# Closing stage of a layer-norm, linear-attention and mixture-of-experts kernel: shared-down and attention products per token tile, and the order of the closing sums

## What is computed

```python
x = L0_attn_x                                   # (1, 1024, 256) float32
xn = _layernorm(x, axis=-1)
x = x + _L0_attn_ref(xn, ...) + _L0_ffn_ref(xn, ...)

# attention: q, k, v = split(xn @ w_qkv); q, k = elu(.) + 1, 16 heads of 16
# running_kv, running_ksum = scans over time of k * v and k, with a decay per head
out = q * running_kv / den
out = out.transpose(0, 2, 1, 3).reshape(B, T, Hid) @ w_out

# feed-forward: each token goes to the best of 8 experts, and all go through a shared one
routed = (h @ wd of the token's expert, gate applied to its input)
shared = _silu_mul(x @ shared_gate_up) @ shared_down
return (routed + shared)
```

## Time and profile before

| | us |
|---|---|
| median of 3 runs | 133.48 |
| lowest and highest of them | 133.03 to 133.86 |
| profiled execution, its own time | 132.86 |
| its span, first to last instruction | 131.2 |
| TensorE busy | 124.0 (94%) |
| VectorE busy | 76.2 (58%) |
| ScalarE busy | 50.6 (39%) |
| GpSimd busy | 31.4 (24%) |

### The profile page before, as it was taken

How to read it: one execution, slowest core, us unless ns; L and a number is a source line. 1 busy time by engine, 2 the same in 40 slices (tenths; PEclk the granted TensorE clock), 3 DMA queues, 4 the chain that set the end, 5 groups by cost and what they waited for, 6 DMA issues and landing times.

```text
span 131.2 us, 2388 instructions
## 1 busy us (share of the span) xinstructions
PE 124.0 (94%) x830; PEld 107.5 (82%) x830; DVE 76.2 (58%) x157; ACT 50.6 (39%) x99; POOL 31.4 (24%) x53
## 2 busy tenths in 40 slices
PE   4989999999999999999999999999999999999870
PEld 1258758787888588999998999899999989999670
DVE  0898876999999967783838333635531324023090
ACT  1675796799856445231313131372222231000000
POOL 7803000018887000101010020202020202478300
PEclk9999999999999999999999999999999999999997
DMA  3675999999942202069999999998881111033336
GB/s 102 206 253 114 315 362 226 227 356 386 387 164 80 90 0 65 20 142 311 334 409 362 370 315 322 371 347 285 303 252 40 38 57 50 9 111 106 94 125 200
DMA packets 20036, 27.25 MB, mean 208 GB/s; under 512 B 1356, under 2 KB 16884, under 8 KB 20024
## 3 DMA queue, kind: packets, MB, share of 16 engines
q1 hardware_dynamic: 14056, 21.24, 50.5%
q0 software_dynamic: 1344, 3.43, 8.2%
q10 hardware_dynamic: 4624, 2.43, 6.6%
HBM read 19.90 MB, written 7.19 MB: 206 GB/s over the span
## 4 chain that ended last, share of the span: by engine, by line
PE 86%; DMA 6%; issue 2%; DVE 2%; POOL 1%; ACT 0%; SPq 0%; DVEq 0%; POOLq 0%
PE ps L1042 21%; PE ps L286 10%; PE ps L285 10%; PE ps L287 10%; PE ps L1056 9%; DMA gu<-in_L_ffn_w_gate_up_dram 6%; PE ps L911 5%; PE ps L986 4%; PE ps L917 4%; PE ps L924 4%; PE ps L980 3%; PE ps L972 2%; PE ps L857 1%; DVE x_sb L840 1%; PE ps L963 1%
## 5 line engine op out<-in xcount | busy, mean ns | idle before, releaser
L1042 PE MATMUL ps<-xgT,gu 128*128 128x144 f32 x256 | 34.2, 287 | 0.6 <-DMA gu<-in_L_ffn_w_gate_up_dram 0.6
L1042 PEld LDWEIGHTS ps<-xgT,gu 128*128 128x128 f32 x256 | 32.3, 190 | 1.2 <-issue 1.0
L794 DVE TENSOR_TENSOR wqkv<-rz,ps 128x288 f32<-128x288 f32 x16 | 7.3, 454 | 26.4 <-ACT rz L545 26.3
L418 POOL DMA_DIRECT2D sorted_rows<-yrow x9 | 6.3, 697 | 60.5 <-DVE yrow L789 55.8
L1056 PE MATMUL ps<-wqkv,dn 128*128 128x144 f32 x128 | 17.4, 289 | 0.0
L545 ACT ACTIVATE rz<-ps 128x288 f32<-128x288 f32 x16 | 6.6, 410 | 26.5 <-PE ps L1042 26.5
L1056 PEld LDWEIGHTS ps<-wqkv,dn 128*128 128x128 f32 x128 | 16.1, 190 | 0.0
L410 POOL DMA_INDIRECT sorted_rows<-xn,slot_row x8 | 11.2, 1397 | 19.2 <-ACT xn L483 17.7
L285 PE MATMUL ps<-xT_hi,sgu_hi 128*128 128x512 f32 x32 | 13.0, 405 | 0.0
L287 PE MATMUL ps<-xT_hi,sgu_lo 128*128 128x512 f32 x32 | 12.5, 391 | 0.0
L286 PE MATMUL ps<-xT_lo,sgu_hi 128*128 128x512 f32 x32 | 12.5, 390 | 0.0
(11 more groups left out here) (146 smaller groups left out, 217.8 us busy)
## 6 DMA issues: line engine op xcount, KB each, us to landing
gu<-in_L_ffn_w_gate_up_dram SPq DMA_DIRECT2D x8, 1024.0 KB, 6.1
dn<-in_L_ffn_w_down_dram SPq DMA_DIRECT2D x8, 512.0 KB
sorted_rows<-zeros SPq DMA_DIRECT2D x1, 2592.0 KB, 16.7
wqkv<-sorted_rows SPq DMA_DIRECT2D x10, 144.0 KB
sorted_rows<-yrow POOLq DMA_DIRECT2D x9, 144.0 KB, 4.0
sgu<-_ffn_shared_gate_up_dram SPq DMA_DIRECT2D x1, 1024.0 KB, 6.1
rden_rows<-rden ACTq DMA_DIRECT2D x1, 1024.0 KB, 14.0
ksum<-rden_rows ACTq DMA_DIRECT2D x2, 512.0 KB, 8.1
```

What stands on the lines that cost most here:

```text
L794: V.tensor_tensor(hr[:, 2 * h:2 * h + 2, :].rearrange("p f s -> p (f s)"), act_sb[:, h, 0:2 * SLOTS], ps[:, 2 * h + 1, 0:2 * SLOTS], ALU.m ...
L1042: ins = mm(ps[:, 2 * h + u, (f % 2) * SLOTS:(f % 2 + 1) * SLOTS], gu[p][:, kc, col:col + P], xgT[:, kc, :], start=(kc == 0), stop=(kc == K ...
```

## The change

TensorE: the two loops become one. For each token tile the 12 shared-down matmuls are followed by the 6 attention matmuls of that tile. The two waits that stood ahead of the second loop stand ahead of the joined one.

VectorE: the order of the 16 closing sums is written out. Tiles 0 to 5 take the dense sum first and then the rows sum, tiles 6 and 7 the rows sum first. The sum that comes first increments `s_sum`, the second `s_fin`, so that each tile is still stored after its second sum. The order is: dense 0, 1, 2, rows 0, dense 3, rows 1, 2, dense 4, rows 3, 4, dense 5, rows 5, 6, dense 6, rows 7, dense 7. The numbers of matmuls, sums, gathers and stores stay as they were.

```diff
-            for i in range(NT + TH):
-                if i < NT:
-                    dve.wait_ge(s_gather[i], 16)
-                    V.tensor_tensor(x_sb[:, i, :], x_sb[:, i, :], y_tok[:, i, :], ALU.add).then_inc(s_sum, 1)
-                if i >= TH:
-                    dve.wait_ge(s_acc, i - TH + 1)
-                    dve.wait_ge(s_sum, i - TH + 1)
-                    V.tensor_tensor(x_sb[:, i - TH, :], x_sb[:, i - TH, :], ps[:, i - TH, 0:D], ALU.add).then_inc(s_fin, 1)
+            ROWS_FIRST = NT - 2
+
+            def dense_add(i):
+
+                dve.wait_ge(s_acc, i + 1)
+                if i >= ROWS_FIRST:
+                    dve.wait_ge(s_sum, i + 1)
+                V.tensor_tensor(x_sb[:, i, :], x_sb[:, i, :], ps[:, i, 0:D], ALU.add).then_inc(s_fin if i >= ROWS_FIRST else s_sum, 1)
+
+            def rows_add(i):
+
+                dve.wait_ge(s_gather[i], 16)
+                if i < ROWS_FIRST:
+                    dve.wait_ge(s_sum, i + 1)
+                V.tensor_tensor(x_sb[:, i, :], x_sb[:, i, :], y_tok[:, i, :], ALU.add).then_inc(s_sum if i >= ROWS_FIRST else s_fin, 1)
+
+            for i in range(3):
+                dense_add(i)
+            rows_add(0)
+            dense_add(3)
+            rows_add(1)
+            rows_add(2)
+            dense_add(4)
+            rows_add(3)
+            rows_add(4)
+            dense_add(5)
+            rows_add(5)
+            rows_add(6)
+            dense_add(6)
+            rows_add(7)
+            dense_add(7)
@@
             pe.wait_ge(s_shl, LAST)
-            pe.wait_ge(s_plo, 1)
+            pe.wait_ge(s_plo, 2)
+            pe.wait_ge(s_attl, KC)
             for i in range(NT):
@@
                 shared_down(i, range(FC))
-            pe.wait_ge(s_plo, 2)
-            pe.wait_ge(s_attl, KC)
-            for i in range(NT):
                 attention_out(i)
```

## The result

| | median us (lowest to highest, runs) |
|---|---|
| before | 134.19 (132.57 to 137.25, 23) |
| changed | 133.34 (131.88 to 137.05, 23) |
| ratio | 0.9929, 95% interval 0.9901 to 0.9956 |

The medians are of all runs and the ratio of the fast ones alone (a run over 1.5% above the kernel's fastest counts as slow), and the profiled execution of the changed kernel was a slow one, 137.05 us.

What follows compares the result with a forecast made beforehand. TensorE was taken to set the pace, then late dense sums, eleven sums in a row and queued stores; ending at 129.1 instead of 131.24 gains 2.1 us off 133.48: 131.4, set at 131.5 for possibly withheld completions, range 130.9 to 133.0.

Steps and rivals of the forecast that it cites:

- the stutter: In TensorE's second loop, late matmul starts put the last at 126.92 instead of 125.78, costing 1.15 us.
- rival B: TensorE's stutter stays, at a place in its instruction stream: gain 0.7 to 1.3 us, time 132.2 to 132.8, chance 0.25.
- What bounds the stage: Closing stage: a late start of the dense sums, eleven sums in a row, and a queue of stores follow each other.
- the withheld completions: VectorE's dense sum of tile 0 waited 3.17 us for TensorE, until 124.42, though its last matmul had ended at 121.03.
- Rival D: At the end, the last matmul's completion is withheld 3.4 us: end at 132.5 instead of 129.1, time 134.7, chance 0.05.
- Moved waits at nothing: TensorE's waits moved ahead of the joined loop cost nothing: operands ready at 93.2 and 77.7, loop starts at 108.63.
- VectorE's sums beside the gathers at nothing: Dense sums in the time of the gathers cost GpSimd nothing: an overlapped gather took 0.95 us, one without 1.05.
- Stores cost a gather 0 to 0.5 us: New stores in the time of the gathers: one store delays a gather 0 to 0.5 us; taken as 0.
- The end behind the last matmul: Last matmul complete 126.06, sum to 126.50, store issued 126.57, landing 1.8 to 2.4 us, then 0.4: 128.8 to 129.4.
- Rival C: Timed runs have no stall, so before has less to lose: gain 0.25 to 0.85 us, 132.6 to 133.2, chance 0.20.
- The range: Whole kernel: 130.9 to 133.0 us, meant to leave out no more than 2 in 10.

Runs made afterwards that it cites:

- the early store: The whole change, with the last store of expert rows, for which the gathers wait, issued from ScalarE's queue instead of GpSimd's; ratio 0.9938, once more 0.9843.

## Why the prediction was wrong

The step that failed is this one: "In the new order at most two increments fall in any 3.2 us, so I expect TensorE not to starve." I had read the stutter as a limit of four open increments, from one trace, and even there the first two late starts (0.21 us apart instead of 0.12, at +14.25 and +14.46) fall with three open. In the first profile of the changed kernel two completions are open when the issue gives out, and it lost 1.7 us, more than before; with the early store one is open. The count of open increments is not what sets it, and where in the stream they fall is not either: without the gathers the same 144 matmuls lose nothing (17.44 us), and the stall moves when the gathers do. With that, 1.15 us or more of the 2.1 fell away, as rival B has it: 0.7 to 1.3 us, measured 0.95. B's time was right by luck, its reason was not: it gave the stutter a fixed place in the stream, and the runs show that it follows the gathers.

The other steps, in their order:

- **What bounds the stage.** Right: the chain through TensorE, the sums and the stores. What I called strange, the withheld completions, was the main thing, and without gathers the same stage takes 20.0 us. I saw that the stall ended within 0.2 us of the last gather's landing and used it only against D, not for a theory of its own; that would have had the stall in both kernels.
- **Moved waits at nothing.** Right: 20.03 us and no gap in both kernels with plain loads.
- **VectorE's sums beside the gathers at nothing.** Right as to issue: the gathers keep 0.95 us and 1.25 us apart. The comparison that I drew it from showed nothing, for the 1.05 us belong to the first gather of a row: with the sums alone no rows sum ran beside the gathers, and they took 1.05 and then 0.95 us all the same. No row shows a part in it for the port pair that the Trainium skill speaks of (SBUF — State Buffer, "Who interferes with whom").
- **Stores cost a gather 0 to 0.5 us.** Wrong in one of two traces of the changed kernel: rows 6 came 2.7 us later than planned. What delayed it is not shown; stores and gathers were both slow there.
- **The end behind the last matmul.** Right and a little pessimistic: 2.6 us from the last completion to the end of the span in the first trace of the changed kernel and in nine of the ten that had no stutter (in the tenth, the change once more, rows 6 came late), where I had 2.7 to 3.3. The last store of the changed kernel, which comes alone, took 1.7 us and not the 2.1 that I put between 1.8 and 2.4.
- **Rival C.** Its sum for before without a stall, 129.65, so 21.0 us, would have been bound by the gathers at 124.6; in the run the plain loads came 6 us earlier, and the stage took 20.0, so the sum itself was not tested. Its point, that the timed runs might have no stall, is refuted: with plain loads in place of its gathers the kernel before gains 2.0% in them.
- **Rival D.** It did not happen as put: no profile shows the last completion of the changed kernel withheld by more than 0.05 us. With the gathers 3.2 us later it did (1.2 us, +17.98 to +19.16), but rows 7, which starts at +19.60, came later still, so it did not set the end.
- **The range.** It ended at 133.0 because it was built on a median of three runs. The 23 runs of before spread from 132.57 to 137.25, so the baseline alone was good for 0.7 us.

What stays open is which part of the chip the whole-row gathers hold. The runs exclude GpSimd's waits, its issuing of DMAs as such and the indirect form alone; the bytes alone are excluded only for loads that are over in 6 to 7 us. In the traces that have the delay, the first completion to be withheld falls 5.6 to 6.8 us after the first gather's issue (8.0 and 8.3 with the loops of before, where none falls earlier), and those up to 4.6 us after it are on time; a pause after four gathers prevents it. Why it takes the completions in one run and the landings in another was not found.

A late fetch of instructions is a rival that the traces can tell about. The seventh 16 KB packet of the instruction queue q8 starts at +13.9 to +14.3 in the nine traces without a stutter and with punctual landings. In the first trace of the changed kernel, in that without GpSimd's waits and in that of the joined loop alone it comes only at +23.5, +23.6 and +20.0, behind the last matmul. All 144 matmuls had been issued by then, so TensorE did not lack what that packet brings; with the early store the issue gives out at +12.8, before the packet is due. Why the packet is late there is open too.

## What to carry to other kernels

When a wait ends in the trace at the same moment as something it does not name, take that coincidence for the first theory and ask where it falls in the changed kernel, before pricing the change as if the wait were gone. A reordering that shortens the line behind a stall is worth at most that line, 1.4 us here, and not the stall. Take the suspected neighbour away, or break its row with one wait: a pause of 2 us in GpSimd's gathers, with an earlier start to pay for it, brought 0.6% and 1.2% on top of the change's 0.7%. And when a stand-in replaces the neighbour, give it the same length in time, or the comparison leaves a rival.

## What was not expected of the hardware

- A row of eight indirect gathers of 128 x 1 KB, 1.25 us apart, kept VectorE from seeing TensorE's completions for 3 to 5 us (121.03 to 124.42 in before, 123.75 to 128.72 in the changed kernel), and TensorE's issue gave out 9.1 to 10.7 us after the first gather's issue, for 0.5 to 1.8 us in all. In one trace of the changed kernel the gathers' own landings were late instead. The same gathers with 256-byte rows did not do it, nor did plain loads of the same bytes from GpSimd or ScalarE, 0.5 us apart.
- In the time of such a hold the gathers' landings and VectorE's increments were seen at once (rows 5 at +13.4 and rows 6 at +14.8, tile 4's completion held from +10.97 to +15.82).
- Six such gathers withheld one completion for 1.9 us and cost no time; four, a landing waited for, and four more withheld at most 0.2 us.
- The Trainium skill gives some 26 ns for an increment (TensorE: Matmul & The Clock Gate, "The cost: per-tile semaphore tail"). That has no part in this: without gathers every dense sum starts 0.03 to 0.04 us after its completion, and nothing adds up over the eight.
